# Second pre-activation matmul behind the seventh first layer, sixth gelu in front of the input's high part, second mask in front of the residual

## The reference, cut to what matters

```
h = tok(x, ...)                                  # counts and a small projection
h = h + attention(layernorm(h), E, Dx, Dy)       # a decaying linear recurrence with 256 states
h = h + experts(layernorm(h), ...)               # 8 experts, each 64 -> 128 -> gelu -> 64, top 2 weigh

# attention, one step:
x_t   = 0.97 * x_state + relu(v_prev @ Dx.T);  x_t /= sum(|x_t|)
y_t   = relu(ln(rho @ x_t) @ Dy.T) * relu(x_t)
v_star = ln(y_t @ E.T);  rho = 0.97 * rho + ln(v_prev) x_t^T
# experts, each of 8: w[e] * (gelu(xn @ W1[e] + b1[e]) @ W2[e] + b2[e]), and the sum over e
```

## Time and profile before

| what | value |
|---|---|
| median of 3 runs | 698.47 us (698.41 to 698.85) |
| the profiled execution | 698.65 us, span 696.9 us |
| PE busy | 636.0 us, 91% |
| PEld busy | 428.5 us, 61% |
| DVE busy | 552.2 us, 79% |
| ACT busy | 436.6 us, 63% |
| POOL busy | 341.8 us, 49% |
| granted PE clock, 160 to 640 us | 1.00 |

### The profile page before, as it was taken

One profiled execution on the slowest core, in us unless ns is written; L12 is line 12 of the kernel. 1 busy time (PEld: TensorE's weight loads), 2 busy tenths in 40 slices (PEclk: granted clock), 3 DMA queues, 4 the chain that ended last, 5 costly groups with the idle time before them and its releaser, 6 DMA issues.

```text
span 696.9 us, 19160 instructions
## 1 busy us (share of the span) xinstructions
PE 636.0 (91%) x5027; PEld 428.5 (61%) x5064; DVE 552.2 (79%) x1956; ACT 436.6 (63%) x1385; POOL 341.8 (49%) x440
## 2 busy tenths in 40 slices
PE   1582997989999999999999999999999999999986
PEld 0472774456666666666666666666666666667542
DVE  4998888976688888888788888887888888887574
ACT  6980997024566666666666666666666666666663
POOL 2000001933465665566666665566656655666552
PEclk9999998899999999999999999999999999999999
DMA  6200000011434444444445444444444444454444
GB/s 214 98 0 1 1 0 1 25 40 35 94 92 102 99 99 99 112 111 109 111 110 117 117 101 99 99 99 99 99 99 99 99 99 114 106 111 100 94 80 84
DMA packets 61295, 60.41 MB, mean 87 GB/s; under 512 B 21796, under 2 KB 56724, under 8 KB 60756
## 3 DMA queue, kind: packets, MB, share of 16 engines
q1 hardware_dynamic: 58836, 59.34, 35.7%
q10 hardware_dynamic: 2240, 0.73, 0.5%
q0 software_dynamic: 192, 0.01, 0.0%
HBM read 55.18 MB, written 4.89 MB: 86 GB/s over the span
## 4 chain that ended last, share of the span: by engine, by line
PE 75%; DVE 10%; ACT 8%; issue 5%; ACTq 1%; DMA 1%; SPq 0%; DVEq 0%
PE bank L1461 16%; PE bank L1331 13%; PE bank L1449 7%; PE bank L1450 6%; PE bank L1392 5%; PE bank L1412 4%; PE bank L1353 4%; ACT skill_rows L605 3%; PE bank L1366 3%; PE bank L1237 2%; PE bank L1370 2%; PE bank L1342 2%; PE bank L1188 2%; PE bank L1226 2%; PE bank L1217 2%
## 5 line engine op out<-in xcount | busy, mean ns | idle before, releaser
L605 ACT ACTIVATE skill_rows<-bank,b1T,w_scale 128x512 f32<-128x512 f32 x256 | 195.1, 777 | 60.7 <-PE bank L1450 59.2
L1461 PE MATMUL bank<-skill_rows,w_sb 128*64 128x256 f32 x1024 | 128.6, 383 | 0.0
L453 POOL TENSOR_TENSOR feat_parts<-skill_rows 128x512 f32<-128x512 f32 x62 | 78.9, 1272 | 75.7 <-DVE feat_parts L979 67.8
L1331 PE MATMUL bank<-feat_parts 128*128 128x256 f32 (+1 forms) x512 | 104.4, 337 | 1.4 <-DVE feat_parts L979 0.9
L1461 PEld LDWEIGHTS bank<-skill_rows,w_sb 128*64 128x64 f32 x1024 | 69.1, 137 | 42.5 <-issue 12.9
L1331 PEld LDWEIGHTS bank<-feat_parts 128*128 128x128 f32 x512 | 77.3, 190 | 12.0 <-DVE feat_parts L985 6.5
L1001 DVE SCALAR_TENSOR_TENSOR feat_parts<-bank,feat_parts 128x256 f32<-128x256 f32 x128 | 45.4, 418 | 46.1 <-PE bank L1392 46.1
L979 DVE TENSOR_TENSOR_SCAN feat_parts<-same,feat_parts 128x512 f32<-128x512 f32 x62 | 74.3, 1238 | 0.0
L1072 DVE SCALAR_TENSOR_TENSOR skill_rows<-bank,b2T,feat_parts 128x256 f32<-128x256 f32 x128 | 54.2, 474 | 7.6 <-issue 4.8
L628 ACT ACTIVATE bank<-bank 128x64 f32<-128x64 f32 x128 | 26.7, 221 | 50.9 <-PE bank L1421 50.9
L1072 DVE SCALAR_TENSOR_TENSOR skill_rows<-bank,b2T,skill_rows 128x256 f32<-128x256 f32 x128 | 54.3, 473 | 4.2 <-PE bank L1461 2.9
(11 more groups left out here) (266 smaller groups left out, 1446.1 us busy)
## 6 DMA issues: line engine op xcount, KB each, us to landing
skill_rows<-w_d SPq DMA_DIRECT2D x32, 512.0 KB, 6.5
feat_parts<-w_d SPq DMA_DIRECT2D x32, 512.0 KB, 6.3
same<-factor_d SPq DMA_DIRECT2D x31, 512.0 KB, 5.2
skill_rows<-skill_row_d SPq DMA_DIRECT2D x4, 1024.0 KB, 7.8
out<-o_sb SPq DMA_DIRECT2D x32, 128.0 KB, 4.9
w_sb<-in_L_ffn_W ACTq DMA_DIRECT2D x2, 256.0 KB
w_d<-wT SPq DMA_DIRECT2D x32, 16.0 KB, 1.4
table_k<-table_d SPq DMA_DIRECT2D x9, 2.5 KB
```

What stands on the lines that cost most here:

```text
L453: pool.tensor_tensor(half[:, n, :], tm[:, 2 * n, :], tm[:, 2 * n + 1, :], ALU.add).then_inc(po_half, 1)
L605: act.activation(hid[:, e, :], h_bank[e % 2][:, :], ACT.Gelu, bias=b1T[:, e:e + 1], scale=w1_scale[:, e:e + 1]).then_inc(ac_gelu, 1)
L1331: last = pe.matmul(n_bank[sc % 2][:, 0:SPAN[sc]], xs[:, k, sc * P:(sc + 1) * P], xs[:, k, sc * P:sc * P + SPAN[sc]], start=(k == 0), stop= ...
L1461: last = pe.matmul(z_bank[q % 2][n * D:(n + 1) * D, at:at + S // 2], w2_sb[:, e, :], hid[:, e, n * (S // 2):(n + 1) * (S // 2)], start=Tru ...
```

## The change

It moves three pieces of work, each within the order of its engine; no instruction is added or removed. On ACT `centred_high(r)` goes from behind `gelu(k, 4)` to behind `gelu(k, 5)`, and so also behind `weights_T(t)`. On DVE `diagonal(i, 1)` goes in front of `residual(r)`. On PE `update(i+1, 1)` goes behind `hidden(k, 6)`.

```
@@ ScalarE
                 if mlp:
                     gelu(k, 4)
-                if res:
-                    centred_high(r)
                 if rt:
                     weights_T(t)
                 if mlp:
                     gelu(k, 5)
+                if res:
+                    centred_high(r)
+                if mlp:
                     gelu(k, 6)
                     gelu(k, 7)
@@ VectorE
                 if att:
                     diagonal(i, 0)
+                    diagonal(i, 1)
                 if res:
                     residual(r)
-                if att:
-                    diagonal(i, 1)
                 if rt:
                     logit_sum(t, m)
@@ TensorE
                 if ahead:
                     update(i + 1, 0)
-                    update(i + 1, 1)
                 if mlp:
                     hidden(k, 6, 1 - side)
+                if ahead:
+                    update(i + 1, 1)
```

## The result

The changed kernel takes 708.88 us (median of 4 runs, 708.18 to 710.51), the kernel before beside it 698.66 us. The ratio is 1.0149, interval 1.013 to 1.0168: slower, by 10.2 us. The profiled execution took 709.22 us, with a span of 707.4.

A forecast was written before the change was run, and what follows sets the result against it. PE was taken as the bound, with DVE's scans just under it. Scans losing 28 x 0.54 = 15.1 us, less 4.7 gained by the mask, made +10.4 us: 708.9 us, likeliest case 706 to 713, whole range 695 to 713.

The forecast's parts named there:

- The scans are the bound just under PE's: DVE from y_core to the next turn's scores: PE's gains there count only up to 0.17 us a turn.
- POOL's three instructions move 0.84 us back: POOL's instructions queued behind centred_high start 0.84 us later, over the scans; whichever engine starts second stands.
- The first block: POOL's middle instruction runs when scan 1 wants to start: scan 1 is 0.33 us late instead of 0.08, +0.25.
- The second block: POOL's third instruction gets in between scan 1 and scan 2, for 0.46 us; bounds 0 and 0.46.
- The mask: Second mask ahead of the residual on DVE: PE's wait at scores 2 and 3 goes, 0.15 us a turn, 4.7 us.
- The router's sum: DVE work behind the residual: keeps its place, since mask and residual only change places.
- The gelu's wait: hidden(k, 7) on PE waits 0.22 us for gelu(k, 5); the wait goes, worth at most 0.17 us by itself.
- The pre-activation: update(i+1, 1) on PE, one hidden later: costs and gains nothing, covered by 0.6 us.
- DVE keeps the port: Rival 1, between the two scans: only the first block counts, 2.5 us faster, 696.0 us; chance 0.22.
- POOL keeps it: Rival 2, the port between POOL's own two instructions: scan 1 0.91 us late, 13.8 us slower, 712.3; chance 0.13.
- the scan wins by a hair: Rival 4: POOL slips in only between the scans, 1.2 us slower, 699.7 us; chance 0.10.
- No collision: Rival 3: scans stay at 2.33 us or slip in front, 10.9 us faster, 687.6 us; chance 0.12.

The follow-up runs named there:

- the two halves: Changed kernel with POOL's weighted_input issued as two instructions of 128 columns each: 702.99 us, ratio 1.0067 against the kernel before.
- ScalarE's part: Kernel before with only centred_high moved behind the copy of the weights and gelu 5: 712.95 us against 698.62, ratio 1.0203.
- VectorE's part alone: Kernel before with only the second mask, diagonal(i, 1), moved in front of the residual: 696.55 us, ratio 0.9972.
- the fastest order: Changed kernel with POOL's mean_back and weighted_input put in front of centred_low: 689.6 us, ratio 0.9868 against the kernel before.

## Why the prediction was right, step by step

- *The scans are the bound just under PE's, with 0.17 us of slack.* Right. With 0.08 us less in the scans the kernel before doesn't move; with 0.62 more, gate to scores grows by 0.44, and 0.62 - 0.17 is 0.45.
- *POOL's three instructions move 0.84 us back, onto the scans, and whoever starts second stands.* Right, and shown: taking the three away from the scans turns the loss into a gain, with the other engines' orders unchanged.
- *The first block, +0.25.* Right: 2.66 against 2.41.
- *The second block: POOL gets in between the scans, for 0.46 us.* The choice was right, and it was a choice; the two halves show it. The size was too large: 0.37. I had charged POOL's whole hold, though part of it passes before the second scan is ready: POOL gets in 1.07 us into the first scan (1.21 - 0.14), and the second wouldn't begin before 1.12 (2.33 - 1.21). By this estimate that is 0.05 of the 0.09; the rest is open.
- *The scans' term as a whole, 0.54 a turn and 15.1 us.* Measured 0.44 a turn, 28 x 0.44 = 12.3 us: 2.8 too high, nearly all by the second block (28 x 0.09).
- *The mask, 0.15 us in each of 31 turns, 4.7 us.* This is the term that was mis-sized most, to more than double. Its wait was read off as 1.46 against 0.86 + 0.45, but two such groups in a row take 1.41 with no wait in them. The sign that the prediction named for it, scores 2 and 3 falling to 1.31, did not come: they fell to 1.41. Alone the mask is worth 2.1 us, 2.6 less than forecast. Together with ScalarE's part it is worth 4.1 (712.95 to 708.88; the pre-activation in between is worth nothing), because the wait that it removes has grown there, by 0.09 us a turn. That growth is a term that the prediction doesn't have: ScalarE's part causes it and the mask takes it away again.
- *The sum, 708.9 us.* Right in sign and in mechanism, but its closeness is luck. The loss was put 2.8 us too high and the gain 2.6 us too high, and the two errors cancel: 12.3 - 2.1 is 10.2, the forecast had 15.1 - 4.7 = 10.4.
- *The router's sum stands where it stood.* Nearly, and not without effect, at the same port. `logit_bias` had stood under POOL's `add_halves` in most turns, 1.23 us in the one of the earlier trace rows. In the changed kernel it comes first, by 0.12 us, and takes its own 0.19 (DVE and POOL):

```profile
421.37 0.19 DVE L1027 TENSOR_TENSOR lg<-lg,br_sb 128x32 f32<-128x32 f32 x1
...
421.49 1.27 POOL L457 TENSOR_TENSOR feat_parts<-feat_parts 128x512 f32<-128x512 f32 x1
```

This is the main reason why DVE's busy time grew by only 4.6 us, though its scans grew by 28 x 0.62, some 17. It buys no time: VectorE's part alone has it too (DVE busy 536.6 us), and its turns are shorter only by the 0.05 to 0.08 us of scores 2 and 3.
- *The gelu's wait, worth at most the slack.* Right: gone in the changed kernel and worth nothing there; without the collision gate to scores falls by 0.25 us.
- *The pre-activation, nothing.* Right alone; beside the fastest order no worth is shown.
- *The rivals.* That DVE keeps the port is excluded by the first of the two halves, which got in between the scans. That POOL keeps it is excluded twice: in the changed kernel the first scan got in between `mean_back` and `weighted_input`, and in the two halves the second scan got in ahead of the second half. That the scan wins by a hair is excluded for this change, by 0.15 us. No collision (forecast at 687.6) is what POOL's new order makes, at 689.6: 28 x 0.32 = 9.0 us, where the forecast had 10.9 with the mask at 4.7.

The Trainium skill's rule on the shared port (SBUF — State Buffer, "Who interferes with whom") held for all the pairs above, in both directions. It does not hold for every GpSimd instruction that reads SBUF: under the power that GpSimd computes in the preamble, 20.82 us long, VectorE's instructions with two SBUF inputs ran without waiting for it, a scan of 512 columns in its usual 1.21 us among them (POOL and DVE of the kernel before):

```profile
119.99 20.82 POOL L400 TENSOR_TENSOR u_scale<-u_scale,power_j 128x128 f32<-128x128 f32 x1
...
123.24 0.29 DVE L885 TENSOR_TENSOR upd_sum<-upd_sum,rstd 128x128 f32<-128x128 f32 x1
...
125.26 1.21 DVE L901 TENSOR_TENSOR_SCAN skill_rows<-skill_rows 32x512 f32<-32x512 f32 x1
```

The figure of some 115 ns behind the other's end, which the prediction took from the Trainium skill (SBUF — State Buffer, "A bandwidth-pool intuition that's wrong"), is given there for a DMA whose descriptors GpSimd writes, waiting for a VectorE copy. It doesn't carry over to two compute instructions: by an estimate from that figure each block would have cost 0.26 us more than the 0.33 and 0.37 measured.

## What to carry to other kernels

Moving an instruction moves all that is queued behind its reader: look up what those instructions will then lie over, above all GpSimd instructions like these, which read SBUF, beside VectorE instructions with two SBUF inputs. When such a chain has slack of a tenth of a microsecond, ask first which of the dependents can go ahead of the wait; here that one edit turned 10 us lost into 9 gained. And take a wait from a row that names it, or from the same shapes in the same neighbourhood; a difference of sums of separate rows can be the cost of standing in a row.

## What was not expected of the hardware

- A lead of 0.04 us decides who gets the port: POOL at 415.63 held up a scan of 415.67, and at 629.61 it was itself the second to DVE's 629.57.
- Between two VectorE instructions that follow each other without a wait, a waiting POOL instruction was let in, exactly one; the second half of `weighted_input` stayed out for the whole second scan.
- The profile counts the wait for the port as busy time of the waiting instruction: POOL's 24 us more, all in `weighted_input` (1.53 us in place of 0.61), and DVE's scans of 1.54 us in place of 1.21 are waits.
